# Two transformer layers on 3,136 image tokens: inputs laid out on the host, embedding inside the tile loop, products by blocks of 128 tokens, layer two five tiles behind layer one

## The reference

```python
h = patches(x) @ W.T                                   # 64 x 49 x 192
# layer one: causal attention, relative positions added to the keys
q, k, v = split(h @ w_attn + b_attn)
scores = (q * 0.25) @ (k + rel).T, masked to j <= i
h = layernorm(h + softmax(scores) @ v @ w_proj + b_proj)
# layer two: full attention, its qkv corrected by a routed low-rank part
probs = softmax(h @ Wg.T + bg); combine = top 2 of 8 experts, others 0
delta = 2 * (sum_e combine_e * (h @ A_e.T + ba_e) @ Bm_e.T + combine @ bb)
q, k, v = split(h @ Wqkv.T + bqkv + delta)
h = layernorm(h + softmax(q @ k.T * 0.25) @ v @ Wproj.T + bproj)
```

## Time and profile before

| | |
|---|---|
| median of three runs | 600.43 us (596.56 to 600.67) |
| span of the profiled execution | 597.9 us; its own time is not listed apart from the three runs |
| PE busy | 509.4 us (85%), 4766 records |
| PE weight loads | 420.2 us (70%) |
| DVE busy | 424.2 us (71%), 1405 instructions |
| ACT busy | 340.4 us (57%), 1273 |
| POOL busy | 157.4 us (26%), 224 |
| moved by DMA | 16.93 MB in 17,347 packets, 15,792 of them under 2 KB |

### The profile page before, as it was taken

How to read it: one execution, slowest core, us unless ns; L and a number is a source line. 1 busy time by engine, 2 the same in 40 slices (tenths; PEclk the granted TensorE clock), 3 DMA queues, 4 the chain that set the end, 5 groups by cost and what they waited for, 6 DMA issues and landing times.

```text
span 597.9 us, 14702 instructions
## 1 busy us (share of the span) xinstructions
PE 509.4 (85%) x4766; PEld 420.2 (70%) x4766; DVE 424.2 (71%) x1405; ACT 340.4 (57%) x1273; POOL 157.4 (26%) x224
## 2 busy tenths in 40 slices
PE   3695594995899999899999999998999999999874
PEld 2595584984777777777777777777777777777652
DVE  2331323325578888888888888888888888888854
ACT  2351232313466766667676676766766677676662
POOL 6000000002233333333333333333333333333120
PEclk9599596998799999999999999999999999999995
DMA  9979597110000000000000000000000000000000
GB/s 158 153 131 124 95 133 100 36 32 0 1 3 6 6 5 5 5 5 5 10 5 5 5 5 5 5 5 5 5 10 5 5 5 5 5 5 5 7 11 10
DMA packets 17347, 16.93 MB, mean 28 GB/s; under 512 B 7816, under 2 KB 15792, under 8 KB 17328
## 3 DMA queue, kind: packets, MB, share of 16 engines
q1 hardware_dynamic: 17328, 16.68, 17.3%
HBM read 11.85 MB, written 2.41 MB: 24 GB/s over the span
## 4 chain that ended last, share of the span: by engine, by line
PE 58%; DVE 15%; issue 9%; DMA 7%; ACT 5%; SPq 5%; DVEq 0%; ACTq 0%
PE ps L556 10%; PE ps L572 9%; PE ps L546 6%; PE ps L471 6%; DMA h_all<-hstage 6%; PE ps L533 4%; PE ps L582 4%; PE ps L601 4%; PE ps L592 3%; ACT pt L781 2%; PE ps L537 2%; PE ps L530 2%; DMA xb<-in_x 2%; DVE hw L1042 2%; SPq L304 1%
## 5 line engine op out<-in xcount | busy, mean ns | idle before, releaser
L415 POOL TENSOR_TENSOR raw<-qk,headmask 128x784 f32<-128x784 f32 x64 | 96.9, 1514 | 119.9 <-DVE k L987 110.9
L965 DVE TENSOR_REDUCE sum<-probs 113x4 f32<-113x196 f32 (+1 forms) x128 | 55.2, 452 | 26.6 <-ACT probs L745 26.5
L471 PE MATMUL ps<-tokw,xt 128*112 128x192 f32 x336 | 65.4, 349 | 0.8 <-ACT xt L713 0.8
L781 ACT COPY pt<-ps 113x339 f32<-113x339 f32 x128 | 53.3, 443 | 18.9 <-PE ps L582 18.8
L775 ACT COPY vbd<-ps 49x96 f32<-49x96 f32 x256 | 60.0, 234 | 2.2
L471 PEld LDWEIGHTS ps<-tokw,xt 128*112 128x112 f32 x336 | 58.8, 192 | 1.5 <-issue 1.2
L948 DVE TENSOR_REDUCE mx<-ps 113x4 f32<-113x196 f32 (+1 forms) x128 | 53.2, 455 | 7.9 <-PE ps L533 7.2
L425 POOL COPY h_all<-h1s 98x192 f32 (+1 forms) x32 | 11.0, 344 | 178.8 <-DVE h1s L1013 178.8
L601 PE MATMUL ps<-p,yt 97*98 97x192 f32 (+1 forms) x256 | 56.0, 341 | 2.4 <-ACT yt L788 2.4
L745 ACT ACTIVATE probs<-probs 113x196 f32<-113x196 f32 (+1 forms) x128 | 51.3, 450 | 10.8 <-DVE probs L956 9.6
L533 PE MATMUL ps<-raw,qk 128*49 128x392 f32 x256 | 56.8, 523 | 0.0
(11 more groups left out here) (123 smaller groups left out, 976.6 us busy)
## 6 DMA issues: line engine op xcount, KB each, us to landing
xb<-in_x SPq DMA_DIRECT2D x42, 112.0 KB, 10.2
xb<-in_x SPq DMA_DIRECT2D x14, 336.0 KB, 12.1
out<-o_sb SPq DMA_DIRECT2D x32, 73.5 KB
h_all<-hstage SPq DMA_DIRECT2D x8, 73.5 KB
tokw_raw<-in_L_tok_W SPq DMA_DIRECT2D x1, 576.0 KB, 6.5
h_all<-hstage SPq DMA_DIRECT2D x8, 63.0 KB
h_all<-hstage SPq DMA_DIRECT2D x8, 52.5 KB
h_all<-hstage SPq DMA_DIRECT2D x8, 42.0 KB
```

What stands on the lines that cost most here:

```text
L415: nc.gpsimd.tensor_tensor(L.kbd, L.qk[:, 1, :].rearrange("p (s j) -> p s j", s=SEQ)[:, :, None, :].to_broadcast([F, SEQ, H0, S]), headmask ...
L471: last = nc.tensor.matmul(ps[0:M, 4 + K % 2, 0:E], xt[g % 2][:, kx, k * M:(k + 1) * M], tokw[:, kx, :], start=(kx == 0), stop=(kx == KX - 1))
L781: nc.scalar.copy(L.pt[:, 3 * c:3 * c + 3, :].rearrange("p g i -> p (g i)"), ps[0:PP, L.bs + c, 0:3 * PP]).then_inc(L.pt_ready[c], 1)
L965: nc.vector.tensor_reduce(L.sum[:, lo:hi], L.p[:, lo:hi, 0:S], AX.X, ALU.add).then_inc(L.sum_ready, 1)
```

## The change

The whole of build is rewritten; the arithmetic stays but for the order of sums and for where constants enter.

- The host lays out every input: pixels as 25 blocks of 128x6x128 (block, pixel within a chunk, chunk, token), all weights transposed and with their columns in the order in which they are used, and constants. Positions and the layer-one bias become 50 further rows of the layer-one contraction (w1b, pos).
- Tokens are also cut into 25 blocks of 128 (the last has 64). Embedding, query/key projections, output projections, both normalisations, the transposes of h and the router work by blocks; attention and the value projections work by tiles of 98 tokens. q and k live in rings of six tiles.
- last_tile(b) is the tile in which block b ends, first_use(b) the first tile that needs it. `ending(i)` and `starting(i)` list the blocks of a step. Both are empty in about one step of four.
- There are 39 steps, written out in full, with no hardware loop. Step i holds layer one of tile i and layer two of tile i-5 (its transposed probabilities and values one step later). Steps 0 to 4 have layer one alone, 32 to 38 layer two alone.
- Heads are kept in two halves of 32 feature rows and three groups m. A tile's scores are 12 products of 32 rows, 49 tokens of q and 98 columns (two heads by 49 keys) in place of 3 large ones. The two layers share the score banks 0 and 1 and the banks 2 and 3 behind them.
- Maximum, subtraction, exponent, sum and scaling are one instruction over all 12 heads each. POOL does both normalisations; the masks are two operations of 64x294 elements a tile and layer.
- h stays in SBUF; the DMA into h_all is gone. SP reloads pixel buffers (five of them) as blocks are embedded. The token weights and constants are issued on ACT's queue.

The core of the new code, cut:

```diff
+def ending(i):
+    return [b for b in range(BLOCKS) if last_tile(b) == i]
+def starting(i):
+    return [b for b in range(BLOCKS) if first_use(b) == i]
+STEPS = TILES + D + 2
...
+            for u in range(3):
+                sp.dma_start(xs[:, 0, 2 * u:2 * u + 2], x[0, :, 2 * u:2 * u + 2]).then_inc(x0_loaded[u], 16)
+            sp.dma_start(w1a[:], w1a_in).then_inc(w1a_loaded, 16)
+            load_x(1)
+            sp.dma_start(w1b[:], w1b_in).then_inc(w1b_loaded, 16)
+            sp.dma_start(tail[64:128], pos_in).then_inc(pos_loaded, 16)
...
+            def block_diagonal(L, t, chain):
+                pool.wait_ge(L.qk_ready, block_of(t) + 1)
+                if t >= 2:
+                    pool.wait_ge(scores_done, chain(t - 2) + 1)
+                slot = T * t % RING
+                for e in range(2):
+                    last = nc.gpsimd.tensor_scalar(L.kbd[t % 2][:, e], L.k[:, :, slot:slot + T],
+                                                   kmask[:, e:e + 1], None, ALU.mult)
+                last.then_inc(L.kbd_ready, 1)
...
+            def scores(L, t, chain):
...
+                for m in range(3):
+                    for half in range(2):
+                        for s in range(2):
+                            last = nc.tensor.matmul(
+                                ps[s * PB:s * PB + S, half, m * T:(m + 1) * T],
+                                L.q[32 * half:32 * half + 32, m, slot + s * S:slot + (s + 1) * S],
+                                L.kbd[t % 2][32 * half:32 * half + 32, :, m, s * S:(s + 1) * S],
+                                start=(L is L2), stop=(L is L2 or m == 2))
...
+            for i in range(STEPS):
+                j = i - D
+                if i < TILES:
+                    scores(L1, i, chain1)
+                for b in ending(i - 1):
+                    row_bank = out_project(L1, p1, b, chain1, row_bank)
+                for b in ending(i - 3):
+                    qk_bank = project_qk2(b, qk_bank)
+                if 0 <= j - 1 < TILES:
+                    transpose_probs(L2, j - 1, chain2)
+                if i < TILES:
+                    turn_bank = project_v(L1, i, values1, turn_bank)
+                if 0 <= j - 1 < TILES:
+                    weigh_values(L2, j - 1, chain2)
+                for b in starting(i + 2):
+                    row_bank = embed(b, row_bank)
+                if 0 <= j < TILES:
+                    scores(L2, j, chain2)
+                for b in ending(i - 1 - D):
+                    row_bank = out_project(L2, p2, b, chain2, row_bank)
+                for b in ending(i - 1):
+                    turn_bank = transpose_h1(b, turn_bank)
+                for b in starting(i + 2):
+                    turn_bank = transpose_h(b, turn_bank)
+                    qk_bank = project_qk1(b, qk_bank)
+                if i < TILES:
+                    transpose_probs(L1, i, chain1)
+                if 0 <= j < TILES:
+                    turn_bank = project_v(L2, j, values2, turn_bank)
+                if i < TILES:
+                    weigh_values(L1, i, chain1)
+                for b in ending(i - 2):
+                    transpose_hw(b)
+                for b in ending(i - 1):
+                    route(b)
```

More of the change, by code:

```diff
@@ new lines, in scores @@
+            def scores(L, t, chain):
+                c = chain(t)
+                if c > 0:
+                    pe.wait_ge(sub_ready, c)
+                else:
+                    pe.wait_ge(masks_ready, 1)
+                pe.wait_ge(L.kbd_ready, t + 1)
+                slot = T * t % RING
+                if L is L1:
+                    for half in range(2):
+                        nc.tensor.matmul(ps[:, half, 0:6 * S], ident_bf[:], causal[:], start=True, stop=False)
+                for m in range(3):
+                    for half in range(2):
+                        for s in range(2):
[4 more added lines that the diff above has]
+                                start=(L is L2), stop=(L is L2 or m == 2))
+                last.then_inc(scores_done, 1)
@@ new lines, in weigh_values @@
+            def weigh_values(L, t, chain):
+                c = chain(t)
+                pe.wait_ge(L.v_ready, t + 1)
+                for half in range(2):
+                    pe.wait_ge(pt_ready[half], c + 1)
+                    for s in range(2):
+                        for g in range(3):
+                            last = nc.tensor.matmul(
+                                ps[32 * g:32 * g + 32, 2, half * T + s * S:half * T + (s + 1) * S],
+                                L.vbd[t % 2][:, s, 32 * (3 * half + g):32 * (3 * half + g) + 32],
+                                L.pt[:, 3 * half + g, s * PB:s * PB + S], start=True, stop=True)
+                last.then_inc(pv_done, 1)
@@ new lines, in exponent, with take_v @@
+            def exponent(L, t, chain):
+                c = chain(t)
+                act.wait_ge(sub_ready, c + 1)
+                p = L.p[:, :, 0:S]
+                nc.scalar.activation(p, p, ACT.Exp).then_inc(exp_ready, 1)
+            def take_v(L, t, chain):
+                act.wait_ge(L.v_done, t + 1)
+                if t >= 2:
+                    act.wait_ge(pv_done, chain(t - 2) + 1)
+                elif t == 0:
+                    act.wait_ge(zeros_ready, 2)
+                for e in range(2):
+                    rows = slice(e * PB, e * PB + S)
+                    last = nc.scalar.copy(
+                        L.vbd[t % 2][rows].rearrange("p s (g e d) -> p s g e d", g=6, e=2)[:, :, :, e, :],
+                        ps[rows, 6, 0:E].rearrange("p (s g d) -> p s g d", s=2, g=6))
+                last.then_inc(L.v_ready, 1)
@@ new lines @@
+    order = [part * E + col for m in range(3) for part in range(2) for col in qk[m]]
+    order += [2 * E + (2 * g + e) * 16 + d for e in range(2) for g in range(6) for d in range(16)]
+    is_k = [part for m in range(3) for part in range(2) for _ in range(64)]
+    order = _np.array(order)
+    k_cols = _np.flatnonzero(_np.array(is_k) == 1)
+    wa = a['L0_attn_w_attn'][:, order]
+    w1a = wa[0:128]
+    w1b = zeros(128, 3 * E)
+    w1b[0:64] = wa[128:E]
+    w1b[65:64 + S, k_cols] = _np.tile(a['L0_attn_rel_emb'][0:S - 1], (1, len(k_cols) // 16))
```

1468 lines of the change are left out of this document (560 added, 908 removed).

## The result

The kernel after takes 575.25 us (median of 4 runs, 575.08 to 577.86) where the kernel before, on the same chip, takes 599.17 (596.56 to 600.67). The ratio is 0.9617, 95% interval 0.9578 to 0.9657. The forecast was 530 us. The direction was right, and the size was not: a third of the forecast gain came (24 us of 70). The profiled execution has a span of 576.0 us, where 528 were forecast.

A forecast was written before the change was run, and what follows sets the result against it. TensorE was taken as the bound, with one wait of about 1.25 us a round. Start 26 + fill 47 + 27 rounds x 14.8 (400) + drain 52 + clock 3 = 528 us span, 530 us measured; 8-in-10 range 470 to 592.

The forecast's parts named there:

- (a): Embedding stage at the start removed: 131 us go and 26 come, 105 saved; first scores at 26 us.
- (b): TensorE's work in the loop: 12.3 us a tile, embedding included, plus 0.25 us a round for changes of shape.
- change of shape: TensorE's cost of switching tiling mode between products: 0.08 us for each of three more a round, 0.25 us.
- (c): VectorE's work in the loop: 9.7 us a tile plus waits for the exponent, so VectorE doesn't bind.
- (d): ScalarE's work in the loop: 8.7 us a tile; GpSimd's masks and normalisation under 4.5 us.
- ahead of need: GpSimd's masks and normalisation in the loop: under 4.5 us and finished before other engines need them.
- (e): Loop round set by ScalarE's written order: 16.3 us with every block item, 14.8 us in the mean.
- router 6.4: In the stepped full round, TensorE finishes the router 6.4 us after layer two's scores, right behind value products at 5.75.
- (f): Fill and drain: 47 us for five layer-one steps, 52 us for the drain, 3 us for the lower clock.
- TensorE stays the bound: Rival for the loop: waits are hidden, a round is TensorE's 12.6 us, total 464 to about 480 us; chance 0.26.
- Row strips don't overlap: Rival for the scores: one layer's records cost 2.0 us, a round 16.8 us, total 592 us; chance 0.10.
- The clock falls: Rival: more holes in TensorE's work cost the full clock, 4.4 us more a round, about 670 us; chance 0.07.

The follow-up runs named there:

- x9_all: Kernel after with router, layer-two deviation and probabilities reordered, masks as tensor_tensor products, layer-one normalisation ahead of the next tile's masks: 479.9 us.
- x15_orders_pool: Kernel after with router, layer-two deviation and probabilities reordered, and GpSimd's layer-one normalisation ahead of layer one's masks, masks unchanged: 483.3 us.
- x7_strips: Kernel after with score products reordered so that three neighbours use the same strip: 629.6 us, ratio 1.051.
- x5_masks: Kernel after with GpSimd's masks written as tensor_tensor products with a broadcast operand: 576.6 us.
- x3_pool_order: Kernel after with GpSimd's layer-one normalisation moved ahead of layer one's masks: 575.1 us.
- x2_route: Kernel after with the router product moved behind the next step's layer-one scores, its maximum and exponent moved to fit: 549.5 us.
- x4_lnv: Kernel after with layer two's deviation moved behind ScalarE's copies of values, outputs and router: 550.7 us.
- x11_route_lnv: Kernel after with the router product behind the next scores and layer two's deviation behind ScalarE's copies: 526.6 us.
- x10_orders: Kernel after with router behind the next scores, layer-two deviation behind ScalarE's copies, probabilities ahead of query/key products: 504.5 us.
- x1_busy: Kernel after with 20 filler bf16 products where TensorE waits, in fill and drain only: 575.4 us.
- x6_probs_first: Kernel after with probability transposes and copies moved ahead of the query/key product and copies in both layers: 573.5 us.
- x13_before_en: Kernel before with en written as scalar_tensor_tensor with a tile of ones: 600.45 us, ratio 1.001.

## Why the prediction was wrong in size

**(a) Embedding out of the way: right.** First scores came at 23.2 us (26 forecast, 22 to 32), and 131 us of embedding went.

**(b) TensorE's work: right in sum, in part by luck.** Forecast 12.3 + 0.25 us a tile. Where TensorE sets the loop, in x9_all and x15_orders_pool, a step takes 12.83. Terms that were off cancel in it. Scores cost 0.66 us a layer, to the next group, for 1.0 taken, 0.68 less a step; the bounds were 1.0 and 2.0, so the lower one was too high. 27 ns a record is below the 41 ns that I took from the weight loads of the earlier trace rows, and it hangs on the strips alternating (x7_strips). Against this stand 0.50 us of waits that are left (13 us in steps 5 to 30 of x15_orders_pool), 0.16 of embedding (2.15 us a block for 1.95 taken, 25 blocks for 32 tiles) and 0.3 more.

The change of shape was taken too low. In the rows of x15_orders_pool above, two records of 192 columns take 0.43 us right behind the scores (339.50 to 339.93) and 0.33 behind their own kind (to 340.26). In the whole step ten changes lengthen the distances by 0.11 to 0.22 us each, about 1.5 us together; that is an estimate, the distances on both sides of a change less those inside the groups. I had counted 0.25 us for three changes; part of the others was in the prices taken from rows. The earlier trace rows had it too: 0.49 us for two records of 196 columns from 400.55. The Trainium skill (TensorEngine Tiling (Array Packing), Key Properties) says that a change of mode drains the array, and the trace agrees that each is paid. My estimate from 166 ns a change (the Trainium skill, TensorE: Matmul & The Clock Gate, Single matmul latency) is near the 150 ns measured; that the step came out at 12.83 all the same is the cheap scores' doing.

**(c), (d) The other engines' sums: right.** DVE 292 us (310 forecast), ACT 267 (290), reductions 770 ns (763), en 0.23 us (under 0.4). One price was wrong: GpSimd. I took the masks at 0.6 to 0.7 us and the normalisation at 0.35 to 0.7, from products of two tensors; they are tensor_scalar operations with the scalar from SBUF and cost 1.04 and 1.0 us. Four masks and a normalisation are 5.2 us in a row, and "ahead of need" failed. In the kernel after this is hidden (x5_masks and x3_pool_order change nothing), since later waits set the step. In a better order it costs 21 to 24 us.

**(e) The order in a round: the step that failed in the loop.** The mechanism named was there: TensorE waits for yt and pt, lnv waits for mv with take_y behind it, and mending that gives 16 us of loop time. What I left out is the last line of the order: route waits for hwt of the block before, the last copy on ScalarE. I had put "router 6.4" right behind the value products, so at no wait; it is 1.16 us in step 17, which has the full clock. In full steps x2_route leaves 0.25 us of it (once 2.9), and its steps, 14.43 us in the mean, are near what I had stepped through (14.8): 16.9 for 16.3 in most full steps, 14.7 for 14.9 without layer two's query/key product, 14.8 for 14.6 without the residual, and 11.1 for 12.8 without embedding and combining. With the wait they are 15.45. The forecast also had the full clock in the loop, and that comes and goes with the waits: 34 us at the lower level with this wait, 10 without. A full step was forecast at 16.3 us and is 16.7 to 16.9 in most of x2_route's, 17.85 after at the full clock and 19.4 where the clock falls.

**(f) Fill and drain: the other step that failed.** The end took 94.3 us for 69.8. The drain was counted as attention alone, 8.3 us a step; for three of its steps the last blocks' router, projections and deviations are still in the written order, and TensorE waits for them (2.38, 1.41 and 3.57 us in the rows of the drain). The five steps take 65.1 us for 41.5. 12 of the 25 us are the deviation's place (x4_lnv), 3 more the router's (x11_route_lnv), 4 the probabilities' (x10_orders). About 5 stay in every version and have no experiment; they lie behind the last scores, from which the end takes 17.3 to 17.6 us in each version looked at, for about 10 forecast and 3 for the clock. With the clock at 0.91 (x1_busy) the end is 2 us shorter. The fill's 10 us too much fall to 1.4 with the three orders mended (48.4 against 47).

**The rivals.** "TensorE stays the bound", 464 to 480 us at 0.26, was false for this kernel and describes the mended one: 480 us and 96% busy from 80 to 380 us. "Row strips don't overlap" was false, by the order in which the products are written. With the other order they still overlap in part: 1.29 us a layer to the next group, where the rival had 2.0 and the kernel has 0.66; the kernel as a whole then takes 55 us more (630 for 575), where the rival added 62 to the forecast (592 for 530). "The clock falls" was true in a small measure: 0.95 to 0.97 in the loop. The mean full step is 1.7 us longer than the one at the full clock (19.6 for 17.85), so 12 us over seven of them at most, and it comes with the waits; filling them gave nothing back, taking them away did.

## What to carry to other kernels

Step through a written order with every wait of each item, also the wait for the buffer that it writes, and ask of each copy at the end of an engine's list who needs it next; two items moved in such lists were worth 49 us here, a twelfth of the time, with not one instruction saved. Do so for fill and drain separately, with their own leftovers. An edit that gives nothing alone may be hidden by a later wait: x5_masks, x3_pool_order and x6_probs_first changed the kernel after by 2 us or less, and each gave over 20 once the later waits were gone (of the first two either one, not both). Errors of a forecast can cancel in a sum: TensorE's came out right with scores too dear and changes of shape too cheap.

## What the hardware showed that was not expected

**Alternating strips.** 12 score products, 24 records of 32 rows by 49 columns, take 0.66 us to the next group when neighbouring products lie on different strips, 27 ns a record, and about twice that (1.29 us) when three products in a row share one. The duration of a single record is the same in both, 241 ns in the median; only the distance shows it. The Trainium skill (TensorE: Matmul & The Clock Gate, Part 3) says that tiles on different rows and columns compose; the runs agree, and add that the order of issue decides.

**A change of shape.** About 0.15 us each, ten in a full step of x15_orders_pool (0.11 to 0.22, an estimate from the distances): as much as a layer's scores for every four or five changes.

**A GpSimd scalar from SBUF.** tensor_scalar over 64x294 elements takes 1,042 ns, tensor_tensor with a broadcast operand 691.

**VectorE held by GpSimd.** In the kernel before, en takes 0.60 to 1.32 us in 30 of 32 rounds and ends 0.03 us behind GpSimd's mask product; in the last two rounds, which have no such product, it takes 0.23 us, as in the kernel after. Another form of the operation changes nothing (x13_before_en, 1.32 us in the median; in its rows en ends at 406.00, the product at 405.97). MAX8, which starts within the same product at 404.49, takes 0.15 us. The Trainium skill (SBUF — State Buffer, Two separate sides) has a rule for it: a VectorE operation with two inputs in SBUF, or in its two-port mode, and a GpSimd operation share a pair of ports that one instruction holds to its end. The rows agree, for an operation of 8 columns too.

**The clock follows the waits.** After several pauses of half a microsecond, or one of 1.36 us, the clock went to its lower level for 3 to 7 us, but not each time: step 17 of the kernel after kept it full to its end through 0.66, 0.46, 0.60 and 1.16 us (it fell 2 us behind the last), and two of six full steps of x10_orders kept it through 1.43. The kernel before pauses 1.01 us in the round of the earlier trace rows and has 1.00 from 270 to 571 us. Filler products raised the granted clock from 0.64 to 0.91 in the drain and left the time as it was.
